# A macaron block with Hadamard-transformed FFNs on one core: the first pass with all up steps ahead of all down steps

## What is computed

```python
def ffn(x):
    up_gate = jnp.einsum('bsd,hd->bsh', x, W1)     # 512 -> 2048
    up_lin  = jnp.einsum('bsd,hd->bsh', x, W3)
    hidden  = silu(up_gate) * up_lin
    hidden  = fwht(hidden)                         # length 2048, scaled by 1/sqrt(2048)
    return jnp.einsum('bsh,dh->bsd', hidden, W2)   # 2048 -> 512
x = x + 0.5 * ffn(layernorm(x))
x = x + attn(layernorm(x))      # per token: scores between its 16 heads, softmax, mix, wo
x = x + 0.5 * ffn(layernorm(x))
```

## Time and profile before

| | before |
|---|---|
| median of 3 runs (lowest to highest) | 2688.82 us (2687.78 to 2691.37) |
| the profiled execution's own time | 2686.21 us |
| its span | 2684.4 us |
| PE busy | 2566.9 us (96%) |
| DVE busy | 2012.8 us (75%) |
| ACT busy | 542.2 us (20%) |
| POOL busy | 357.0 us (13%) |

### The profile page before, as it was taken

How to read it: one execution, slowest core, us unless ns; L and a number is a source line. 1 busy time by engine, 2 the same in 40 slices (tenths; PEclk the granted TensorE clock), 3 DMA queues, 4 the chain that set the end, 5 groups by cost and what they waited for, 6 DMA issues and landing times.

```text
span 2684.4 us, 32324 instructions
## 1 busy us (share of the span) xinstructions
PE 2566.9 (96%) x11328; PEld 2093.5 (78%) x11328; DVE 2012.8 (75%) x2482; ACT 542.2 (20%) x829; POOL 357.0 (13%) x171
## 2 busy tenths in 40 slices
PE   4998989999999999999999999999999999998799
PEld 3777768888888888878888888888788888876687
DVE  8556997777777777877777787777777777779812
ACT  1321221121212212112112221112121121112111
POOL 5033880000000000000000000000000000158400
PEclk7999999999999999999999999999999999999899
DMA  5571441555425553355524555155542555234344
GB/s 189 194 308 56 163 153 52 184 206 184 177 78 188 203 188 141 111 186 204 188 94 161 184 204 187 70 192 199 187 166 99 184 201 190 109 117 157 118 180 164
DMA packets 91642, 437.02 MB, mean 163 GB/s; under 512 B 8896, under 2 KB 15296, under 8 KB 58304
## 3 DMA queue, kind: packets, MB, share of 16 engines
q1 hardware_dynamic: 83616, 420.65, 43.1%
q10 hardware_dynamic: 7968, 15.73, 1.6%
HBM read 402.79 MB, written 33.55 MB: 163 GB/s over the span
## 4 chain that ended last, share of the span: by engine, by line
PE 69%; DMA 13%; DVE 13%; issue 2%; SPq 1%; POOL 1%; ACT 0%; POOLq 0%; ACTq 0%; DVEq 0%
PE gu L316 17%; PE gu L318 16%; PE gu L317 16%; DMA w_up<-up_pairs 12%; PE acc L316 6%; PE acc L318 6%; PE acc L317 6%; DVE mixed L830 2%; DVE prod L231 2%; DVE scores L828 2%; DVE hid L777 1%; PE gu L354 1%; DVE tok L1007 1%; SPq L297 1%; DVE prod L228 1%
## 5 line engine op out<-in xcount | busy, mean ns | idle before, releaser
L316 PE MATMUL gu<-xt,w_up 128*128 128x512 f32 x2048 | 809.5, 395 | 48.8 <-DVE w_up L981 26.5
L317 PE MATMUL gu<-xt,w_up 128*128 128x512 f32 x2048 | 799.8, 391 | 0.0
L318 PE MATMUL gu<-xt,w_up 128*128 128x512 f32 x2048 | 799.0, 390 | 0.0
L316 PEld LDWEIGHTS gu<-xt,w_up 128*128 128x128 f32 x2048 | 385.7, 188 | 161.7 <-DMA w_up<-up_pairs 47.9
L773 DVE TENSOR_TENSOR gated<-gated,gu 128x512 f32<-128x512 f32 x256 | 175.2, 684 | 428.9 <-ACT gated L530 428.9
L318 PEld LDWEIGHTS gu<-xt,w_up 128*128 128x128 f32 x2048 | 385.9, 188 | 81.6
L317 PEld LDWEIGHTS gu<-xt,w_up 128*128 128x128 f32 x2048 | 386.1, 189 | 77.6
L316 PE MATMUL acc<-w_down,hid 128*128 128x512 f32 x960 | 382.5, 398 | 33.3 <-DVE hid L777 33.3
L530 ACT ACTIVATE gated<-gu 128x512 f32<-128x512 f32 x256 | 153.1, 598 | 1243.1 <-PE gu L318 1243.1
L318 PE MATMUL acc<-w_down,hid 128*128 128x512 f32 x960 | 379.0, 395 | 0.0
L317 PE MATMUL acc<-w_down,hid 128*128 128x512 f32 x960 | 378.8, 395 | 0.0
(11 more groups left out here) (103 smaller groups left out, 2200.4 us busy)
## 6 DMA issues: line engine op xcount, KB each, us to landing
w_up<-up_pairs SPq DMA_DIRECT2D x240, 1024.0 KB, 5.9
w_down<-down_pairs SPq DMA_DIRECT2D x240, 512.0 KB, 3.3
up_pairs<-w_up SPq DMA_DIRECT2D x16, 1024.0 KB, 4.9
prod<-up_raw SPq DMA_DIRECT2D x16, 512.0 KB, 6.0
down_pairs<-w_attn SPq DMA_DIRECT2D x4, 2048.0 KB, 10.6
x_in<-x ACTq DMA_DIRECT2D x7, 1024.0 KB, 5.4
out<-x_out ACTq DMA_DIRECT2D x7, 1024.0 KB, 5.5
tok<-attn_raw SPq DMA_DIRECT2D x4, 1024.0 KB, 12.4
```

Of the source, the lines that this page charges most:

```text
L316: nc.tensor.matmul(o, w_hi, m_hi, start=first, stop=False)
L317: nc.tensor.matmul(o, w_hi, m_lo, start=False, stop=False)
L318: return nc.tensor.matmul(o, w_lo, m_hi, start=False, stop=last)
```

## The change

It concerns the first pass alone.

- PE makes all 16 up steps first, then all 16 down steps. After each of the up steps 7 to 14 it makes a batch of four Hadamard matmuls (`hadamard_batch`): 336 columns after steps 7 to 10, 176 columns after steps 11 to 14.
- DVE does all three cuts of butterflies; POOL does none. They are cut into 24 pieces (a subtraction, or the `2a - b` of one level). `turn(2)` is made before block 0, and one piece follows the multiplication of each block and another ends the block's work, until none is left. The cuts now come in by DMA in the order 0, 1, 2.
- Blocks 0 to 3 are split at once, into `xt[1]`, as before. Blocks 4 to 13 (`RAW`) are stored unsplit, in `x_out`, `x_mid` and `prod[:, 2]`, which are free then, and split during the down steps into the two slots of `hid`. Blocks 14 and 15 stay in `gated` and are split at the start of the down steps.
- The down steps run in the order `DOWN_0`: blocks 0 to 3, 14, 15, 4 to 13. In this order the position is called a place.
- SP makes all 16 `keep_up`s, then the four `keep_down`s and `load_attn`s in turn once all 32 Hadamard results are split, and waits for all of them before it loads weights for the second pass.
- POOL's splits of the attention weights wait for 4, 10, 14 and 16 down steps (before: 4, 8, 12, 16).

```diff
+        SPLIT_FIRST = 4
+        SPLIT_LAST = (HT - 2, HT - 1)
+        RAW = tuple(n for n in range(SPLIT_FIRST, HT) if n not in SPLIT_LAST)
+        DOWN_0 = tuple(range(SPLIT_FIRST)) + SPLIT_LAST + RAW
+        BATCH = 4
+        HADAMARD_FROM = 7
...
-            for c in (2, 0, 1):
+            for c in range(len(W2_CUTS)):
...
+            sp.wait_ge(s_down_hi, 2 * HT)
+            sp.wait_ge(s_down_lo, 2 * HT)
             for m in range(4):
...
+                keep_down(m)
                 load_attn(m)
             for u in range(2):
                 sp.wait_ge(s_up_stored[u], 8 * HT)
+            for m in range(4):
+                sp.wait_ge(s_down_stored[m], 16)
...
+                for n in range(HT):
                     pe.wait_ge(s_up_hi, n + 1)
                     pe.wait_ge(s_up_lo, n + 1)
...
+                    up(n, n % 2, X)
...
+                    for part, a in hadamard_batch(n):
+                        at = HT * part + a
+                        if a == 0:
+                            pe.wait_ge(s_fwht, part + 1)
...
+                for place, n in enumerate(DOWN_0):
+                    down(place, place % 2, place == 0, place == HT - 1, staged(n), hidden_0(place))
...
+            for place, n in enumerate(DOWN_0):
+                if place >= SPLIT_FIRST:
+                    act.wait_ge(s_h, n + 1)
+                    if n in RAW:
+                        act.wait_ge(s_down_done, place - 1)
...
-                pool.wait_ge(s_down_done, 4 * (m + 1))
+                pool.wait_ge(s_down_done, 1 + max(DOWN_0.index(n) for n in range(4 * m, 4 * m + 4)))
...
+            turn(2)
+            for n in range(HT):
+                u = n % 2
+                dve.wait_ge(s_silu, n + 1)
+                nc.vector.tensor_tensor(raw_hidden(n) if n in RAW else gated[:, u, :], gated[:, u, :], gu[:, 2 * u + 1, :], ALU.mult)\
+                    .then_inc(s_h, 1)
+                turn(1)
+                if n + 2 < HT:
+                    up_low(n + 2, u)
+                for part, a in hadamard_batch(n):
...
+                if n < SPLIT_FIRST:
+                    dve.wait_ge(s_hid_hi, n + 1)
+                    high, low = hidden_0(n)
+                    nc.vector.tensor_tensor(low, gated[:, u, :], high.bitcast(FP32), ALU.subtract).then_inc(s_hid_lo, 1)
+                turn(1)
+            angles()
```

More of the change, by code:

```diff
@@ L166, in build, with raw_hidden, hidden, hidden_0 @@
         LAST = TILES - 1
[L167 to L172, removed]
-            return hid[:, u, 0, :], hid[:, u, 1, :]
+        SPLIT_FIRST = 4
[4 more added lines that the diff above has]
+        HADAMARD_FROM = 7
+        def raw_hidden(n):
+            at = RAW.index(n)
+            if at < SUBS:
+                return x_out[:, at, :]
+            if at < 2 * SUBS:
+                return x_mid[:, at - SUBS, :]
+            return prod[:, 2, (at - 2 * SUBS) * TOK:(at - 2 * SUBS + 1) * TOK]
+        def hidden(u):
+            return hid[:, u, 0, :], hid[:, u, 1, :]
+        def hidden_0(place):
+            if place < SPLIT_FIRST:
+                return xt[1][:, 0, place, :], xt[1][:, 1, place, :]
+            return hidden(place % 2)
+        def hadamard_batch(n):
+            at = (n - HADAMARD_FROM) * BATCH
+            if not 0 <= at < 2 * HT:
+                return ()
+            return tuple((at // HT, a) for a in range(at % HT, at % HT + BATCH))
         def raw_slot(m):
@@ L331, in up, with down @@
                 ins.then_inc(s_up_done, 1)
-            def down(n, u, first, last, slab=None):
+            def down(n, u, first, last, slab=None, split=None):
                 pe.wait_ge(s_hid_lo, n + 1)
                 hi, lo = (w_down[:, u, 0, :], w_down[:, u, 1, :]) if slab is None else slab
-                h_hi, h_lo = hidden(n, u)
+                h_hi, h_lo = hidden(u) if split is None else split
                 for s in range(SUBS):
@@ L605, in _ @@
             nc.scalar.activation(cos_t[:, 0:POS], cos_t[:, 0:POS], ACT.Sin).then_inc(s_trig, 1)
-            with act.Fori(EARLY // 2, HT // 2 - 1) as jj:
-                for u in range(2):
-                    ffn_step(2 * jj + u, u, True)
-                    up_high(2 * jj + u + 2, jj + 1, u, True)
-            for u in range(2):
-                ffn_step(HT - 2 + u, u, True)
+            for place, n in enumerate(DOWN_0):
+                if place >= SPLIT_FIRST:
+                    act.wait_ge(s_h, n + 1)
+                    if n in RAW:
+                        act.wait_ge(s_down_done, place - 1)
+                    nc.scalar.activation(hidden_0(place)[0], raw_hidden(n) if n in RAW else gated[:, n % 2, :], ACT.Copy)\
+                        .then_inc(s_hid_hi, 1)
             act.wait_ge(s_attn_raw[O], 16)
@@ L775, in h_and_low @@
                 dve.wait_ge(s_hid_hi, n + 1)
-                high, low = hidden(n, u)
+                high, low = hidden(u)
                 nc.vector.tensor_tensor(low, gated[:, u, :], high.bitcast(FP32), ALU.subtract)\
@@ L1064, in normed @@
+            angles()
+            for place, n in enumerate(DOWN_0):
+                if place >= SPLIT_FIRST:
+                    dve.wait_ge(s_hid_hi, place + 1)
+                    high, low = hidden_0(place)
+                    nc.vector.tensor_tensor(low, raw_hidden(n) if n in RAW else gated[:, n % 2, :], high.bitcast(FP32), ALU.subtract)\
+                        .then_inc(s_hid_lo, 1)
             def normed(s):
```

220 lines of the change are left out of this document (80 added, 140 removed).

## The result

| | before | changed |
|---|---|---|
| median (lowest to highest) | 2688.30 us (2682.96 to 2691.37, 4 runs) | 2661.01 us (2657.65 to 2663.74, 4 runs) |
| ratio, 95% interval | | 0.9901 (0.9886 to 0.9916) |
| span of the profiled execution | 2684.4 us | 2655.9 us |
| PE busy | 2566.9 us | 2562.9 us |
| POOL busy | 357.0 us | 318.4 us |

What follows compares the result with a forecast made beforehand. PE was taken as the bound, with 33.8 us of first-pass loss to win. Work 134.8 + entry and slack 1.0 + new waits 3.9 = 139.7 against 168.6 us, 28.9 less: 2660 us, range 2654 to 2670.

Steps and rivals of the forecast that it cites:

- The old wait and its slow clock: Before up step 2: PE's 26.5 us wait for an up weight and 3.05 us of slow clock go whole.
- Does up step 2 start in time: First up steps: block 2's low half is ready at about 28.5 us, against its use at 29.06.
- The term of 1.0 for the entry and the slack: Up steps: 1.0 us charged for up step 2's start and DVE's slack under 1 us together.
- DVE follows PE: Up steps: without POOL's butterflies DVE needs about 5.4 us a step early on, level with PE's 5.44.
- Hadamard matmuls: Batches between up steps: the same 15.15 us of PE, nothing charged for changes between kinds of matmul.
- The splits beside POOL (3.9): Down steps: POOL's attention-weight splits hold DVE's splits, so PE loses 1.8 and 2.1 us, 3.9 in sum.
- rival 3: Down steps: the clock falls after both new waits, each costing about 3.05 us, giving 2666 us; chance 0.05.
- as long as before: Behind the last down step: the stretch was to take no longer than in the kernel before.
- SP's queue: Down steps: 12.6 MB of stores and loads take 29 us, less than the 43.5 of the down steps; nothing charged.
- rival 4: Up steps: transfers bound them, decisive below 210 GB/s; at 163 GB/s 59 us too long, 2719 us; chance 0.04.
- Rival 5: Up steps: the hold only moves to the 16th butterfly piece before the Hadamard matmuls, time stays 2689 us; chance 0.03.
- the slower side: Whole kernel: slower by more than 0.2% (5.4 us), chance 0.04.

Runs made afterwards that it cites:

- the early additions: Changed kernel with two more DVE additions of 512 elements behind each of blocks 1 to 6: 2671.69 us.
- everything stored twice: Changed kernel with every up weight stored twice in the first pass, 1 MB more for each block: 2688.69 us.
- the hold alone: Changed kernel with POOL's last subtraction (low half of wo) held until the layer norm behind the first pass is written: 2659.47 us.
- the tensor alone: Changed kernel with the second DRAM tensor of the doubled stores declared, but only one 1 MB store into it: 2662.36 us.
- the late additions: Changed kernel with two more DVE additions of 512 elements behind each of blocks 8 to 13: 2661.76 us.
- The two runs without the waits: Changed kernel without POOL's q, k and v weight splits, 2652.99 us; changed kernel with q and k splits in eight pieces on ACT and DVE, 2655.34 us.
- pieces and hold: Changed kernel with q and k splits in pieces on ACT and DVE, and POOL's last subtraction held until the norm is written: 2650.37 us.

## Why the prediction was right, step by step

- **The old wait and its slow clock (29.5 us).** Right: both gone whole. The 26.5 us came from DVE's butterflies being slow beside POOL's: they are gone when POOL's part is taken out of the old order, and 18.6 us of waiting are back when it is put into the new one.
- **Does up step 2 start in time.** Right, barely, and partly luck: the low half came at 28.6 us, forecast 28.5, its use at 28.7. When the same kernel ran again the raw weight landed 1.1 us later, PE waited 0.9, and silu 2 came at 35.55 instead of 34.43. The term of 1.0 for the entry and the slack then does not cover the up steps: silu 1 to silu 7 took 34.4 us instead of 33.4.
- **DVE follows PE.** Right: 5.5 us a step against 5.44. The charge of 1.0 for the entry and the thin slack was a little small: up steps 2 to 7 lost 0.7, the entry to the Hadamard batch 0.7, and 14 up steps with all batches took 92.1 us, of which 76.2 + 14.1 are work, so 1.8.
- **Hadamard matmuls.** Charged with 15.15. In batches they took 4 x (7.75 - 5.44) + 4 x (6.65 - 5.44) = 14.1: 1.0 too much, which hid the 0.8 too little above.
- **The splits beside POOL (3.9).** The step that was worth most after the first. Place, mechanism and size right: 1.88 and 1.96 us at places 6 and 12 (forecast 1.8 and 2.1), place 11 in time, the third split without harm. Counted from matmul to matmul the two cost about 2.2 us each. The Trainium skill (SBUF — State Buffer, "Who interferes with whom") says that a DVE instruction with two SBUF inputs contends with a GpSimd one that reads SBUF. The rows of the splits agree, and so do the sums with an input in PSUM, which took 0.67 us each beside POOL's subtraction, as they did before without it. The prediction added that an instruction with a single SBUF input does not contend. That holds for the sums, but the norm's four `tensor_scalar` on `x_in` took 6.08 us beside POOL and 1.92 without.
- **The term that was missing: the clock.** It stood as rival 3 with 0.05 and came true in part. In both profiles of the changed kernel it fell once, after the second wait, for 3.4 us, which costs 1.7. In six other runs with the same two waits (POOL's butterflies back, the early additions, everything stored twice, the Hadamard matmuls last, the hold alone, the tensor alone) it fell after both, as the rival said; in the run with the late additions it fell after the second alone. A fall costs 1.7 us, not the 3.05 of the rival. Behind the norm the lower level then lasted into the projections, so that from the last down step to the rope it took 22.5 us instead of 20.2: another 2.3, where "as long as before" had been forecast. The two runs without the waits had this back, but with pieces and hold the lower level lasted into the projections without any such wait, so that the waits bring it is not shown. The chance was too low. The trace of before showed both outcomes in the second pass, a wait of 2.52 us with the clock at full level behind it and one of 2.30 with matmuls at the lower level. Being busy around it was no protection. This is the mis-sized part of the forecast: a term put at nothing that measured 1.7 us in the down steps and 2.3 behind them. The rows of the two waits before:

```profile
304.89 0.50 PE L316 MATMUL acc<-w_down,hid 128*128 128x512 f32 x1 [2.52 <-DVE hid L777]
...
324.37 0.79 PE L316 MATMUL acc<-w_down,hid 128*128 128x512 f32 x1 [2.30 <-DVE hid L777]
324.96 0.63 PE L317 MATMUL acc<-w_down,hid 128*128 128x512 f32 x1
```

- **SP's queue, and rival 4.** The forecast took nothing, rightly: the stores ended in the down steps. The estimate that transfers decide only below 210 GB/s was too comfortable, though. Doubling the stores shows that the raw weights' landing time, not the mean rate, is what ACT meets, and the 1.1 us in the changed kernel run again show it without any added store.
- **Rival 5** and the slower side fall with the waits above.

The sum, from silu 1 to the end of the last down step: 142.1 us against a forecast 139.7. The clock's 1.7 is most of the difference. In the profiled execution the second pass begins 24.4 us earlier (its first silu at 229.11, before at 253.51), 23.6 when run again, where 28.9 had been promised. The median came out nearly as forecast since the rest of the program scatters by more than this: from that silu to the end it takes 2430.9 us before, 2426.8 in the profiled execution of the changed kernel, and 2431.4 in the one run again. In the profiled execution two errors of some 4 us on either side met. Of the 27.3 us between the medians some 24 are thus seen in the first pass, and where the other 3 come from no trace here shows. The 1 us between forecast and median is in part luck, and not a measure of how well the steps were known.

## What to carry to other kernels

Before work is given to POOL beside DVE, add up what both take together: here POOL's twelve instructions of 39 us in all made DVE's first butterflies and one up weight some 25 us longer (before, 16.1 to 54.3 us, against the same instructions alone), where doing the work itself costs DVE 13 us. Where instructions with two SBUF inputs must run beside POOL, put them where the engine that waits for them has work for the length of POOL's whole instruction, or cut the instruction into pieces that fit in idle time. And a wait of 2 us on PE should be charged with the clock that may fall behind it (1.7 us here, after 15 of 18 such waits), and not only with its length.

## What was unexpected of the hardware

- Four butterfly pieces of 336 elements beside POOL cost 11.66 and 11.94 us, some 6.7 times their 1.76 alone, while one piece of 1344 elements cost 2.60 against 1.56 (3.80 for a subtraction of that size with POOL's part put back). Here several short instructions with two SBUF inputs suffered more than one long one.
- The clock can fall behind a PE wait of 1.88 to 2.37 us with PE busy on either side, 0.7 to 1.5 us after the wait's end, and it need not: of nine runs with both waits it fell after the second in all and after the first in six. And it stayed at the lower level through 16 transposes and into the projections, till 190 us in the changed kernel, where before it had risen as they began.
- With 16 MB more written in the first 130 us, PE waited 33.9 us for weights in the rest of the program instead of 12.1 to 17.4, and the rest took some 18 us longer. A tensor of that size at the same place that got a single store of 1 MB did not do this. The cause is open.
